# Two-layer graph transformer on one core: seven block products in the first experts' second product, and three sums moved in the fourth attention layer

## The reference

```
# first layer, feed-forward: 2 of 4 experts are chosen for the whole input
h = einsum('bld,edh->belh', x, w1) + b1        # 768 -> 1536
h = stack([gelu, silu, mish, gelu][e](h[:, e]))
out = einsum('belh,ehd->beld', h, w2) + b2     # 1536 -> 768
y = einsum('be,beld->bld', gate, out) + x      # then a layernorm with gain and bias
# second layer, attention (one head)
w = exp(leaky_relu(e_src[src] + e_dst[dst]) - m[dst])
out = segment_sum(h[src] * (w / z[dst])) + b
```

## Time and profile before

| | |
|---|---|
| time, median of 3 runs | 2616.97 us (2616.96 to 2617.95) |
| the profiled execution: its time | 2616.33 us |
| its span, first to last instruction | 2614.6 us |
| PE busy | 2541.4 us (97%) |
| DVE busy | 1623.4 us (62%) |
| ACT busy | 769.6 us (29%) |
| mean granted clock of TensorE | 0.993 |
| first experts, 1000 to 1630 us: PE, DVE busy | 620.71, 534.03 of 630 us |
| fourth attention layer and around, 2104 to 2390 us: PE, DVE busy | 278.92, 145.98 of 286 us |

### The profile page before, as it was taken

One profiled execution on the slowest core, in us unless ns is written; L12 is line 12 of the kernel. 1 busy time (PEld: TensorE's weight loads), 2 busy tenths in 40 slices (PEclk: granted clock), 3 DMA queues, 4 the chain that ended last, 5 costly groups with the idle time before them and its releaser, 6 DMA issues.

```text
span 2614.6 us, 26620 instructions
## 1 busy us (share of the span) xinstructions
PE 2541.4 (97%) x10544; PEld 1805.1 (69%) x10544; DVE 1623.4 (62%) x2762; ACT 769.6 (29%) x1291; POOL 347.4 (13%) x197
## 2 busy tenths in 40 slices
PE   7999999999999997999999999999999999999999
PEld 4667667658966996777777775465755786556676
DVE  4456472789948996987878998254442470663422
ACT  1143343006732863222222221430001431342000
POOL 0888888100000000000000000000000000000000
PEclk9999999999999998999999999999999999999999
DMA  8232313543020406000120002200360100213201
GB/s 258 25 45 14 50 2 50 138 155 120 20 80 21 117 1 216 1 1 1 73 103 1 24 24 89 97 1 1 86 187 26 37 1 1 59 36 133 87 24 59
DMA packets 139167, 160.73 MB, mean 61 GB/s; under 512 B 96618, under 2 KB 108484, under 8 KB 137516
## 3 DMA queue, kind: packets, MB, share of 16 engines
q1 hardware_dynamic: 68323, 158.60, 19.5%
q0 software_dynamic: 70720, 0.43, 2.8%
HBM read 122.75 MB, written 35.87 MB: 61 GB/s over the span
## 4 chain that ended last, share of the span: by engine, by line
PE 51%; DVE 7%; ACT 2%; issue 1%; DMA 0%; SPq 0%; DVEq 0%; ACTq 0%
PE psum L526 50%; DVE arena L1958 2%; ACT arena L1154 1%; ACT arena L1159 1%; DVE arena L1960 1%; DVE arena L1959 1%; PE psum L537 1%; DVE arena L1951 0%; ACT arena L1043 0%; DVE arena L1547 0%; DVE arena L2024 0%; DVE arena L1389 0%; DVE arena L1957 0%; DVE arena L1950 0%; DVE arena L1983 0%
## 5 line engine op out<-in xcount | busy, mean ns | idle before, releaser
L526 PE MATMUL psum<-arena 128*128 128x250 f32 (+11 forms) x9712 | 2440.4, 413 | 37.6 <-DMA arena<-in_ffn_w 7.2
L526 PEld LDWEIGHTS psum<-arena 128*125 128x125 f32 (+3 forms) x9712 | 1710.1, 188 | 743.8 <-issue 141.0
L2373 POOL DMA_INDIRECT count_matrix<-arena x170 | 342.8, 2016 | 120.9 <-DVE arena L1486 59.7
L1958 DVE RECIPROCAL arena<-arena 128x500 f32<-128x500 f32 x60 | 196.7, 3278 | 2.1
L1641 DVE CUSTOM_DVE_ANT_0 arena<-arena 125x1250 bf16<-125x1250 bf16 (+1 forms) x100 | 139.2, 1456 | 11.7 <-DMA arena<-source_rows 7.1
L2383 POOL MEMSET arena<- 125x60 f32 x1 | 0.2, 211 | 1040.1 <-PE psum L526 1040.1
L1726 DVE TENSOR_TENSOR arena<-arena 125x1250 f32<-125x1250 f32 x80 | 116.2, 1453 | 12.9 <-ACT arena L1136 12.2
L1133 ACT ACTIVATE arena<-arena 125x1250 f32<-125x1250 f32 x80 | 106.9, 1336 | 54.4 <-PE psum L526 54.3
L1729 DVE SCALAR_TENSOR_TENSOR arena<-arena 125x1250 f32<-125x1250 f32 x80 | 116.9, 1461 | 2.8
L1276 ACT ACTIVATE arena<-psum,arena 128x250 f32<-128x250 f32 x120 | 49.3, 466 | 199.7 <-PE psum L526 199.7
L1086 ACT ACTIVATE arena<-arena 32x500 f32<-32x500 f32 (+1 forms) x108 | 59.1, 548 | 164.8 <-DVE arena L1520 163.9
(11 more groups left out here) (243 smaller groups left out, 1477.7 us busy)
## 6 DMA issues: line engine op xcount, KB each, us to landing
arena<-in_ffn_w SPq DMA_DIRECT2D x3, 4608.0 KB, 14.6
residual<-arena SPq DMA_DIRECT2D x30, 336.0 KB
arena<-residual SPq DMA_DIRECT2D x30, 336.0 KB
arena<-target_rows SPq DMA_DIRECT2D x12, 610.4 KB
arena<-in_gat_w SPq DMA_DIRECT2D x3, 2304.0 KB, 10.7
arena<-residual SPq DMA_DIRECT2D x10, 672.0 KB
residual<-arena SPq DMA_DIRECT2D x10, 672.0 KB
count_matrix<-arena SPq DMA_DIRECT2D x2, 3125.0 KB, 26.6
```

What stands on the lines that cost most here:

```text
L526: return pe.matmul(o, lhsT, rhs, start=start, stop=stop, skip_group_check=share)
L1958: now(dve.reciprocal(t_, t_))
L2373: pool.indirect_dma_start(counts[k], bass.IndirectOffsetOnAxis(ap=IDX_I[0:T, c:c + 1].bitcast(U32), axis=0), COUNT_I[0:T, c:c + 1], None, ...
```

## The change

Second product of the first experts (`down0`): of the 12 blocks of hidden channels, channels 0 to 5 (blocks of three by two column halves, and two tiles) are now multiplied by seven block products of 3 matmuls instead of eight; channels 6 to 11 stay as they were (`rest`). Per unit there are 21 + 24 matmuls in four banks d, b, c, a. VectorE now reads eight times per unit, four of them between parts (`parts_filled`, `parts_read`). It has to make sums of the hidden values for each unit (`sums_of_hidden`) and of the weights once per expert (`weight2_sums`). The activation's algebra is changed to make room: ScalarE takes an exp and then a square of each piece, into two small buffers `EB`, and VectorE needs four operations on a piece instead of six and a clamp. VectorE's reads of the banks of unit u-1 stand between the pieces of unit u, and the last two of them (c and a) behind the joining, the sums and `pair_residual`. `WQ` is loaded in two parts, the second after bank b of unit 9, and the three constant rows of the mixer behind it.

Fourth attention layer: `scale(2, 0)` and `scale(2, 1)` stand a pair later, inside `spread(g)` behind the read of bank b; the first `block_sums` stands ahead of the wait for the last tile of features, in another place of the arena; and the first product waits for the first five tiles alone.

```diff
-            V.extend(("f2", u - 1, i) for i in range(4))
+            V.extend(("f2", u - 1, i) for i in "dbca")
@@ TensorE
-                pe.wait_ge(a_drained, A_AT[("h", layer, NT - 1, 1)] + 1)
+                pe.wait_ge(a_drained, A_AT[("h", layer, 4, 1)] + 1)
...
+                product(1, bank_a, True).then_inc(parts_filled, 1)
+                pe.wait_ge(hidden_sums, u + 1)
+                pe.wait_ge(w2_sums, u // 5 + 1)
+                product(5, bank_b, True).then_inc(parts_filled, 1)
+                rest(1, 1, bank_d, True)
+                pe.wait_ge(parts_read, n + 1)
+                product(6, bank_a).then_inc(parts_filled, 1)
+                pe.wait_ge(parts_read, n + 2)
+                product(3, bank_b, False, False)
+                rest(0, 1, bank_b)
+                pe.wait_ge(parts_read, n + 3)
+                product(7, bank_a).then_inc(parts_filled, 1)
+                product(2, bank_c, True, False)
+                rest(0, 0, bank_c)
+                pe.wait_ge(parts_read, n + 4)
+                product(4, bank_a, False, False)
+                rest(1, 0, bank_a)
@@ ScalarE
-                    act.wait_ge(clamped, 6 * u + i + 1)
-                    act.activation(EB[:, 2 * i:2 * i + 2, :], TB[:, 2 * i:2 * i + 2, :], ACT.Exp).then_inc(expd, 1)
+                    if n >= 2:
+                        act.wait_ge(exp_read, n - 1)
...
+                    act.activation(x, HB[u % 2][:, 2 * i:2 * i + 2, :], ACT.Exp, scale=SCL[:, e:e + 1]).then_inc(act_step, 1)
...
+                    act.activation(x, x, ACT.Square, bias=MISH[:, e:e + 1]).then_inc(expd, 1)
@@ VectorE, a piece
+                dve.tensor_scalar(t_, EB[n % 2], BIG, 1.0, ALU.min, ALU.add).then_inc(exp_read, 1)
+                dve.wait_ge(exp_read, n + 1)
+                now(dve.reciprocal(t_, t_))
+                now(dve.tensor_scalar(t_, t_, c(NCK), c(KO), ALU.mult, ALU.add))
+                ins = dve.tensor_tensor(t_, t_, h, ALU.mult)
@@ VectorE, the loop
+                    pieces = 2 if u == 1 else 4
+                    for i in range(pieces):
+                        if (u, i) == (6, 2):
+                            weight2_sums(1)
+                        ratio(u, i)
...
+                if 7 <= u < 10:
+                    pair_residual(u - 7)
...
+                if u > 0:
+                    add_bank(u - 1, "c", 0, 0)
+                    add_bank(u - 1, "a", 1, 0)
@@ VectorE, spread(g)
+                    if g > 2:
+                        scale(2, g - 3)
                     if g < 4:
                         weights(n, g + 1)
...
-                        if t in (5, 7):
-                            scale(2, t // 6)
@@ SyncE
-                    load(WQ, w["mix1_wq"], m1w[0])
+                    load(WQ[:, 0:5], w["mix1_wq"][:, 0:5], m1w[0])
+                    vf(("f2", 9, "b"))
+                    load(WQ[:, 5:6], w["mix1_wq"][:, 5:6], m1w[0])
+                    for k, name in ((1, "mix1_bo"), (2, "mix1_bk"), (3, "mix1_bv")):
+                        row_load(k, name, m1_small)
```

More of the change, by code:

```diff
@@ L48 @@
 SLOPE = 0.2
+BIG = 1.0e30
+GATED_PARTS = 60
+SPREAD_PARTS = 40
 H0, C0 = 4, 192
@@ L295, in gps_kernel @@
         CO = small(16)
+        KO, MISH, CC, NCK, KG, SCL = (CO[:, 2 * i:2 * i + 2] for i in range(6))
         IS = small(2, 4)
@@ L807, in _, with down0, blocks, product @@
             mm(b[:, 0:4], ONES[:, 0:1].to_broadcast([128, 128]), POOLC[:, 0:4], True, True).then_inc(v_filled, 1)
+            def down0(u):
+                low, high = slice(0, 3), slice(3, 6)
+                tile = [slice(0, T), slice(T, 2 * T)]
+                h = HB[u % 2]
+                col = [slice(0, HALF), slice(HALF, D)]
+                def blocks(x):
+                    return [x[:, e] for e in range(3)]
+                s3 = [HS3[0][:, 0], HS3[1][:, 0], HS3[1][:, 1]]
+                left = [blocks(h[:, low, tile[0]]), blocks(h[:, high, tile[0]]), s3, blocks(h[:, high, tile[1]]),
+                        blocks(HS0), blocks(HS1), blocks(h[:, low, tile[1]])]
+                right = [W2[:, low, col[0]], W2[:, high, col[0]], W2[:, high, col[1]], W2T[2], W2T[0], W2T[1],
+                         W2[:, low, col[1]]]
+                bank_d, bank_b, bank_c, bank_a = (fill("V", ("f2", u, i)) for i in "dbca")
+                n = 4 * u
+                def product(i, b, begin=False, end=True):
+                    for e in range(3):
+                        last = mm(b[0:T, 0:HALF], left[i - 1][e], right[i - 1][:, e, :], begin and e == 0, end and e == 2,
+                                  share=True)
+                    return last
+                def rest(tt, half, b, begin=False):
+                    for m in range(6, HM):
+                        last = mm(b[0:T, 0:HALF], h[:, m, tile[tt]], W2[:, m, col[half]], begin and m == 6, m == HM - 1,
+                                  share=True)
+                    last.then_inc(v_filled, 1)
+                product(1, bank_a, True).then_inc(parts_filled, 1)
[15 more added lines that the diff above has]
+                rest(1, 0, bank_a)
@@ L826, in _ @@
                     pe.wait_ge(act_made, u)
-                    for i in range(4):
-                        tt, half = divmod(i, 2)
-                        b = fill("V", ("f2", u - 1, i))
-                        for m in range(HM):
-                            last = mm(b[0:T, 0:HALF], HB[(u - 1) % 2][:, m, tt * T:(tt + 1) * T],
-                                      W2[:, m, half * HALF:(half + 1) * HALF], m == 0, m == HM - 1)
-                        last.then_inc(v_filled, 1)
+                    down0(u - 1)
             def q1(c):
```

184 lines of the change are left out of this document (115 added, 69 removed).

## The result

| | before | after |
|---|---|---|
| median | 2617.46 us (2616.96 to 2618.99, 4 runs) | 2599.07 us (2598.17 to 2599.93, 4 runs) |
| span of the profiled execution | 2614.6 us | 2597.2 us |
| PE: busy, matmul records | 2541.4 us, 10544 | 2521.6 us, 10484 |
| DVE busy | 1623.4 us | 1561.5 us |
| ACT busy | 769.6 us | 815.0 us |

The ratio is 0.9932, with a 95% interval of 0.992 to 0.9944: 0.7% faster. The forecast was 2599.0.

The account below looks back on a forecast made before the run. TensorE, busy 97% of the span, was taken as the bound. 9.65 us saved in the experts and 8.36 in the attention make 18.0: from 2616.33 to 2598.3, or 2599.0 as a median, range 2592.5 to 2607.

Parts of the forecast that it names:

- The 30 matmuls: Second product of the first experts: three matmuls fewer in each of ten units, 0.645 us each, save 19.35 us.
- VectorE's piece: Activation in the first experts: four operations on a piece take 5.04 us instead of 6.99, 12 us a unit less.
- 3.8 us of slack: Middle unit of the first experts: VectorE reads the first part at 34.3 us, and TensorE wants it read at 38.1.
- Some 8 us a unit more to spare: First experts: VectorE, after its new sums and reads, has some 8 us a unit more to spare.
- Unit 6: First experts: the second expert's weight sums delay the unit's first bank read to 39.7 instead of 38.1, 1.6 us lost.
- Ahead of unit 9: Before unit 9's second product: bank c read late, TensorE idle 5.1 us (4.6 more than before), 2.5 us of cold clock.
- The queue: End of the experts: three constant rows delay `BQ1` by 3.4 to 4.8 us against 2.5 of slack; 1.0 us lost.
- part of it hides in the 2.5 us of cold clock: End of the experts: of the 0.9 to 2.3 us delay of `BQ1`, part hides in the cold clock; 1.0 us taken.
- The attention layer: Fourth attention layer: TensorE's waits of 1.46 and 4.15 us go, with 2.75 of cold clock: 8.36 us saved.
- of the first: Rival, chance 0.15: milder waits in the experts, with VectorE's piece below 5 us; 4.6 us better, 2594.
- A piece takes 5.34 instead of 5.04: 2607: Rival, chance 0.20: short hand-overs in the experts pile up, with the clock falling at unit 6 too; 8 us worse.
- the third rival: Chance 0.04: VectorE becomes the bound in the experts; from a piece of about 5.7 us the change is slower.

Follow-up runs that it names:

- mm_48: The changed kernel with three more matmuls of 125x384 per unit in bank d, so 48 a unit again: 2619.81 us.
- u6_three: The changed kernel with three pieces instead of four ahead of unit 6's first bank read: 2598.20 us.
- c_first: The changed kernel with bank c of the last unit read ahead of `pair_residual`: 2592.64 us.
- warm: The changed kernel with seven matmuls of 125x384 more on TensorE ahead of unit 9's second product, while it waits for bank c: 2599.07 us.
- rows_last: The changed kernel with the three rows of constants issued behind `BQ1` and ScalarE waiting for `BQ1` alone: 2598.58 us.
- bq_first: The changed kernel with `BQ1` loaded ahead of the mixer's weights `WK` instead of behind them: 2599.60 us.
- piece_2: The changed kernel with two more passes over 128x500 on VectorE in every piece, behind the reciprocal: 2627.27 us.
- piece_1: The changed kernel with one more pass over 128x500 on VectorE in every piece, behind the reciprocal: 2613.26 us.

## Why the prediction was right

- **The 30 matmuls.** 19.35 us. Shown by `mm_48`, where they come back at their full duration within 0.4 us; a middle unit takes 59.39 us (59.4 predicted).
- **VectorE's piece.** 4.93 us measured, 5.04 predicted; the last product takes 0.60 from its start to the next piece where 0.72 was counted, and the rest is as counted. No middle unit waits, even with 0.45 us more a piece, so at least 1.8 of the 3.8 us of slack walked for the first hand-over are there. "Some 8 us a unit more to spare" was too much, without effect: the prediction's own terms give 7.1 us less work in a unit that is 1.9 shorter, and from last read to last read VectorE is busy 40.98 of 59.39 us now and was busy 48.35 of 61.32, 5.4 us more to spare. By this cut of the unit it had 13 us to spare before, not the 9 of the earlier trace rows.
- **Unit 6.** 1.61 us, predicted 1.6; the read and not the sums (`u6_three`).
- **Ahead of unit 9.** 4.82 us idle and 2.2 us of cold clock, predicted 5.1 and 2.5; the place of bank c's read (`c_first`), and the idle as the cause of the clock (`warm`).
- **The queue.** A wait of 1.53 us where 1.0 was taken. The rows' own delay is as predicted (`rows_last`: 4.3 us). That the slack of 2.5 us read from the kernel before still held is luck: pair 3's store came 7.1 us later, and the queue behind it was 6.0 us quicker without the rows. And the step "part of it hides in the 2.5 us of cold clock" was wrong. The queue that ends in `BQ1` hangs on TensorE too: in the changed kernel and in every variant of it, with the cold clock and without (`warm`), pair 3's store is issued 8.64 or 8.65 us ahead of the mixer's first matmul, so nothing hides. What differs is the time from that store to the bias: 23.99 us in the changed kernel, 24.28 in `u6_three`, 24.85 in `c_first`, 25.30 in `mm_48` and 25.42 in `warm`, with TensorE's waits of 1.53, 1.82, 2.39, 2.83 and 2.96 us. Why it differs stays open.
- **The attention layer.** 8.50 us, predicted 8.36; 6.77 for the scale's move (predicted 6.9). In the trace after, VectorE comes to the scale at 2337.13 and waits for nothing there.
- **The sum.** 9.42 + 8.50 = 17.9 us in the two stretches, 18.0 predicted. In the experts the measured terms give 19.35 - 1.61 - 4.26 - 2.2 - 1.53 = 9.75, 0.3 above the stage's 9.42; the errors of 0.3 us each in the idle ahead of unit 9 and in the cold clock went one way and that of 0.5 in the queue the other, so the sum is closer than its terms.
- **The rivals.** None came true as a whole; of the first, the piece below 5 us did, for the reason given. One was mis-sized. "A piece takes 5.34 instead of 5.04: 2607" is too low: with 5.38 it is 2613.3, since the clock falls at four places and not two. So VectorE is too slow from an earlier point than the 5.7 us of the third rival: between the 2613.3 of 5.38 and the 2627.3 of 5.83 us the 2617 of before lie at about 5.5, an interpolation. The margin that the change lived on was 0.6 us a piece, where 5.7 would have left 0.8.

## What to carry to other kernels

Where one engine is the bound, walk a single period of the schedule with durations from the trace, and then every place at which the period is broken: the first, the one with extra work in it, and the last. Here the middle was free, and all loss sat in three places: the unit with extra work, the last unit, and the start of the next stage. Each was mended by a change of order alone.

Where a term is a slack read from the kernel before, ask whether each end of it stays in place. Here one end moved by 7 us, and only a second move hid that.

When a saved wait gives nothing, look for the next consumer of the same late thing before calling the gain unreal: `bq_first` and `warm` gained 0.2 and -0.5 us alone, and `warm` gained 2.1 once the queue was in order.

Every wait of TensorE in these stages of 2.42 us or more also cost 1.4 to 2.9 us of cold clock behind it; count that for each, not once.

## What was not expected of the hardware

Whether the clock falls behind an idle of some 2 us is not settled by the idle's length. It stayed at 1.00 behind waits of 1.61 us (changed kernel), 2.39 (`c_first`) and 2.41 (`piece_2`); behind the last two, 36 records took 15.36 us. It fell behind 2.42 (`piece_1`, 16.84 us for the same records), 2.83 (`mm_48`) and 2.96 (`warm`, 17.05 in both), but also behind one of 2.05 us in `piece_2` and one of 1.88 us in the kernel before, ahead of 914.89. Nor does it always fall within the idle. In `piece_1` TensorE began again at 1385.78, behind 3.79 us:

```profile
1385.80:1387.80 2.00, 2.00 (x5) 1.18 (x6) 1.97 (x3) 0.00 (x0) 0.00 (x0) 0.73 0.00 0
1387.80:1389.80 2.00, 2.00 (x5) 1.08 (x4) 2.00 (x1) 0.00 (x0) 0.00 (x0) 0.50 0.00 0
```

A mean of 0.73 over 2 us, with 0.50 behind it, is about 0.9 us of work at the full clock and then the fall. The fall behind unit 9's idle cost 2.2 us in the changed kernel, 1.4 in `u6_three` with the same idle of 4.82 us ahead, and 2.9 in `mm_48` with 4.66. What decides between them stays open.
